# Cross-attention of a decoder layer: heads on 64 array rows each, maxima alternating with scores, weighted sums two at a time, all batches written out

## The reference, cut to what matters

```python
x = x + attn(layernorm(x), wq, wk, wv, wo)                 # 2 heads of 64, rotary, causal, 256 tokens
# cross-attention: B = 4, S = 256 queries, 1601 keys, 16 heads of 8
Q = split_heads(query @ Wq + bq); K = split_heads(key @ Wk + bk); V = split_heads(value @ Wv + bv)
scores = jnp.einsum('bhqd,bhkd->bhqk', Q, K) / sqrt(8)
attn = jax.nn.softmax(scores, axis=-1)
ctx = jnp.einsum('bhqk,bhkd->bhqd', attn, V)
x = x + (ctx.transpose(0, 2, 1, 3).reshape(4, 256, 128) @ Wo + bo)
x = x + ffn(layernorm(x), W1, b1, W2, b2, scale)           # 512 hidden, gelu, a low-rank term of the tokens
```

## Time and profile before

| what | value |
|---|---|
| time of three executions | 507.9, 504.13, 505.81 us, median 505.81 us |
| span of the profiled execution, first to last instruction | 502.5 us (its own device time is not given apart) |
| busy PE / DVE / ACT / POOL | 447.6 / 351.7 / 299.8 / 58.1 us |
| instructions | 10204 |
| mean granted TensorE clock | 0.929 of full |

### The profile page before, as it was taken

One profiled execution on the slowest core, in us unless ns is written; L12 is line 12 of the kernel. 1 busy time (PEld: TensorE's weight loads), 2 busy tenths in 40 slices (PEclk: granted clock), 3 DMA queues, 4 the chain that ended last, 5 costly groups with the idle time before them and its releaser, 6 DMA issues.

```text
span 502.5 us, 10204 instructions
## 1 busy us (share of the span) xinstructions
PE 447.6 (89%) x3264; PEld 197.8 (39%) x3264; DVE 351.7 (70%) x829; ACT 299.8 (60%) x608; POOL 58.1 (12%) x55
## 2 busy tenths in 40 slices
PE   1755899999899998999999997999999999999956
PEld 1542133445333434455333334455333435333224
DVE  3773988885969784786978882876878886892041
ACT  1411057676576756586677746586677648778811
POOL 3500000370000000460000000460000000000000
PEclk9856579999999999999999999999999999999956
DMA  6064720042032201051141202051140200000000
GB/s 223 3 223 127 207 90 2 1 149 99 27 117 70 74 5 47 34 191 57 31 142 39 77 1 82 1 198 50 33 151 30 77 1 12 1 2 0 1 0 12
DMA packets 18884, 33.80 MB, mean 67 GB/s; under 512 B 1424, under 2 KB 16400, under 8 KB 18832
## 3 DMA queue, kind: packets, MB, share of 16 engines
q1 hardware_dynamic: 18832, 33.10, 20.1%
HBM read 17.33 MB, written 11.93 MB: 58 GB/s over the span
## 4 chain that ended last, share of the span: by engine, by line
PE 68%; DVE 16%; issue 6%; DMA 5%; ACT 3%; SPq 1%; POOL 1%; DVEq 0%; POOLq 0%; ACTq 0%
PE wsum L976 18%; PE score L994 17%; PE ring L1010 15%; DVE part_max L634 8%; DMA q_unit<-q_rows 2%; PE ring L1145 2%; PE ring L1114 2%; PE ring L1107 2%; PE ring L1053 2%; DMA q_rows<-q_parts 2%; PE ring L1043 2%; PE ring L1021 1%; PE ring L1150 1%; PE ring L1157 1%; PE ring L1137 1%
## 5 line engine op out<-in xcount | busy, mean ns | idle before, releaser
L634 DVE TENSOR_REDUCE part_max<-ring 128x1 f32<-128x401 f32 x512 | 260.6, 567 | 81.4 <-PE ring L1010 80.2
L848 ACT ACTIVATE probs<-score 128x512 f32<-128x512 f32 (+1 forms) x416 | 224.8, 598 | 71.4 <-PE score L994 70.1
L1010 PE MATMUL ring<-k_unit,q_unit 96*128 96x401 bf16 x512 | 143.1, 355 | 7.2 <-DMA q_unit<-q_rows 6.3
L994 PE MATMUL score<-q_unit,k_unit 128*128 128x512 bf16 (+1 forms) x416 | 128.6, 390 | 5.4 <-issue 5.0
L976 PE MATMUL wsum<-probs,v_unit 128*32 128x256 f32 (+1 forms) x1664 | 130.6, 391 | 0.6 <-ACT q_unit L859 0.6
L1010 PEld LDWEIGHTS ring<-k_unit,q_unit 96*128 96x128 bf16 x512 | 48.6, 100 | 96.4 <-issue 25.5
L976 PEld LDWEIGHTS wsum<-probs,v_unit 128*32 128x32 f32 (+1 forms) x1664 | 34.2, 108 | 64.5 <-issue 42.0
L994 PEld LDWEIGHTS score<-q_unit,k_unit 128*128 128x128 bf16 (+1 forms) x416 | 31.6, 100 | 68.1 <-ACT probs L848 49.2
L859 ACT ACTIVATE q_unit<-ring 3x1024 bf16<-3x1024 bf16 x16 | 16.3, 1017 | 31.4 <-PE ring L1021 30.9
L595 POOL TENSOR_TENSOR var<-mv,c_sb 128x2 f32<-128x2 f32 x4 | 0.8, 197 | 228.7 <-DVE mv L784 228.7
L563 POOL TENSOR_TENSOR k_parts<-k_full,c_sb 128x802 bf16<-128x802 f32 x7 | 10.7, 1524 | 132.9 <-ACT k_full L894 132.9
(11 more groups left out here) (105 smaller groups left out, 316.0 us busy)
## 6 DMA issues: line engine op xcount, KB each, us to landing
k_unit<-k_rows SPq DMA_DIRECT2D x32, 300.2 KB
v_unit<-v_aug SPq DMA_DIRECT2D x16, 234.0 KB, 5.7
ctx_sb<-ctx_t SPq DMA_DIRECT2D x4, 800.5 KB, 6.3
k_rows<-k_parts SPq DMA_DIRECT2D x4, 601.5 KB, 3.3
k_rows<-k_parts SPq DMA_DIRECT2D x4, 599.2 KB, 3.7
k_rows<-k_parts SPq DMA_DIRECT2D x4, 401.0 KB, 4.1
k_rows<-k_parts SPq DMA_DIRECT2D x4, 399.5 KB, 4.3
q_unit<-q_rows SPq DMA_DIRECT2D x32, 48.0 KB
```

The source lines that it names most:

```text
L634: v_.tensor_reduce(part_max[:, par, q, head, hp, c:c + 1], ring[s][:, 0:CW], AX.X, ALU.max)\
L848: a_.activation(probs[0:rows, i % PB, :], score[i % EB][0:rows, :], ACT.Exp)\
L994: mm(score[i % EB][0:keys, :], k_unit[:, u, L * hp + P * t:L * hp + P * t + keys], q_unit[:, u, :, hp, :], start=True, stop=True).then_inc ...
L1010: mm(ring[s][:, 0:CW], q_unit[0:PR, mu, par, hp, P * q:P * (q + 1)], k_unit[0:PR, mu, L * hp + (CW - 1) * c:L * hp + (CW - 1) * c + CW], s ...
```

## The change

The pair of heads is pulled apart. Each half of the array's rows takes one head: rows 0 to 50 and 64 to 114 hold three rows of ones or maxima (`MR`) and the 48 rows of parts. `q_unit` loses its zero blocks. A score step is four matmuls of 256 columns on 51 rows in place of two of 512 on 128; a bank now has both pairs for one head half. Before each score pair stands one M on the other half of the rows. The weighted sums of two keys steps stand together (`PV_AT`). The numbers of M by keys step and unit change (`PAIRS`, `AHEAD`). The rows of ones are loaded once from DRAM, where VectorE set 32 rows of each unit before; the maxima rows of `q_unit` are zeroed by two small DMAs at each load of queries, because the M of a unit reads them too. The hardware loop is gone: all 16 units are written out.

```diff
-AHEAD = (4, 8, 8, 8)
-PR = 2 * TR
+MR = 3
+KR = MR + TR
+HALF = P // 2
-QUOTA = [[5, 5, 5, 5, 4, 4, 4], [5, 5, 5, 5, 4, 4, 4], [6, 6, 6, 4, 2, 0, 4], [7, 7, 6, 6, 2, 4, 4]]
+AHEAD = (4, 16, 14, 8)
+PAIRS = ((1, 1, 1, 1, 1, 1, 2, 1, 1, 1, 1, 1, 2), (1,) * 13,
+         (1, 1, 1, 2, 1, 1, 1, 2, 1, 1, 1, 1, 0), (2, 2, 1, 2, 2, 1, 2, 2, 1, 2, 2, 1, 2))
+TURN_AT = (10, 10, 11, 10)
+PV_AT = {1: (-2, -1), 3: (0, 1), 5: (2, 3), 7: (4, 5), 9: (6, 7), 11: (8, 9), 12: (10,)}
...
+    for t in range(KT):
+        pairs = PAIRS[u][t]
+        for n in range(2):
+            plan += todo[:min(pairs, 1)]
+            todo = todo[min(pairs, 1):]
+            plan.append(("S", v, t, n))
+        plan += todo[:2 * pairs - 2] if pairs > 1 else []
...
+        for at in PV_AT.get(t, ()):
+            if at >= 0:
+                plan.append(("PV", v, at))
+            elif v:
+                plan.append(("PV", v - 1, KT + at))
...
-                    sp.dma_start(q_unit[TR * par:TR * (par + 1), u, par, :, :].rearrange("p h n -> p (h n)"),
+                    sp.dma_start(q_unit[HALF * par + MR:HALF * par + KR, u, :, :].rearrange("p h n -> p (h n)"),
                                  q_rows[b, :, at:at + 2 * DX, :].rearrange("t (d h) n -> t d (h n)", h=2))\
                         .then_inc(unit_in[u], 16)
+                    sp.dma_start(q_unit[HALF * par:HALF * par + MR, u, :, :].rearrange("p h n -> p (h n)").bitcast(F32),
+                                 consts[0:MR, C_COLS["zeros"][0]:C_COLS["zeros"][1]]).then_inc(unit_in[u], 16)
...
-                v_.memset(k_unit[PR:P, u, :].bitcast(F32), TWO_ONES)
-                v_.memset(q_unit[:, u, :, :, :].rearrange("p a h n -> p (a h n)").bitcast(F32), 0.0)\
-                    .then_inc(unit_set, 1)
...
+            def scores(v, t, par):
+
+                u, i = v % UB, score_index(v, t, par)
+                keys = P if t < KT_FULL else LAST
+                rows = slice(HALF * par, HALF * par + KR)
...
+                if i >= EB:
+                    pe.wait_ge(probs_done, i - EB + 1)
+                for hp in range(2):
+                    last = mm(score[i % EB][0:keys, S * hp:S * (hp + 1)],
+                              k_unit[rows, u, L * hp + P * t:L * hp + P * t + keys], q_unit[rows, u, hp, :],
+                              start=True, stop=True)
+                last.then_inc(scores_ready, 1)
+
+            def maximum(item):
+
+                v, k = item[1:]
+                u = v % UB
+                hp, q, c, head = k // (2 * QT * KC), k // (2 * KC) % QT, k // 2 % KC, 1 - k % 2
+                if k == 0:
+                    pe.wait_ge(unit_in[u], 96 * (v // UB + 1))
...
+                s = take(item)
+                rows = slice(HALF * head, HALF * head + KR)
+                mm(ring[s][:, 0:CW], q_unit[rows, u, hp, P * q:P * (q + 1)],
+                   k_unit[rows, u, L * hp + (CW - 1) * c:L * hp + (CW - 1) * c + CW], start=True, stop=True)\
+                    .then_inc(filled[s], 1)
```

669 lines of the change are left out of this document (278 added, 391 removed), and 7 rows, old and new, of tables (PREP_END, PREP_SIDE).

## The result

The changed kernel takes 522.62 us (median of five executions, 518.69 to 530.3), the kernel before 505.81 (five, 503.9 to 507.9): a ratio of 1.032, 95% interval 1.025 to 1.040. It is slower, where 468 us and faster had been forecast. The profiled execution is the longest of the five (530.3 us, span 528.3); in the four others the span was 516.7 to 524.7 us and the mean granted clock 0.841 to 0.862, against 0.835 in the profiled one. What follows accounts for that execution: it is 25.8 us longer than the profiled one of the kernel before (span 502.5), where the medians are 16.8 apart.

A forecast was written before the change was run, and what follows sets the result against it. TensorE was taken as the bound, DVE near. From 502.5 us: three batches -29.7, first unit -4.1, last three -7.0, start +3.0 gave a 464.7 us span; plus 3.3 to the median, 468 us, 80% range 444 to 491.

The forecast's parts named there:

- Row halves: TensorE's keys step: maxima run beside scores on the other row half, so both cost 0.45 us, not 0.88.
- load rival: Keys step: if a weight load's 99 ns is a rate, six loads make it 0.60 us; 482 us, chance 0.12.
- serial rival: Row halves run one after the other on TensorE; a unit's core is 18.7 us; 490 us, chance 0.10.
- Joined sets: Weighted sums in pairs: some 0.2 us saved per avoided return, 7 returns a unit in place of 12 or 13.
- core of 13.3 us: TensorE's scores, maxima and weighted sums in a unit, side work excluded: 13.3 us, 6.6 less than 19.9.
- drift of "some 2 us": Four ring banks and three score banks let the engines drift by only some 2 us.
- rival with chance 0.07: Clock falls to 0.50 part of the time in unit 3: some 3 us a batch, more in unit 2; 478 us.
- unit 0 at 25 us: Unit 0, with the feed-forward: floors TensorE 22.6, DVE 22.3, ACT 20.2 us, plus an allowance for side work, 25 us.
- wait for the queries: Unit 2: TensorE waits 4.7 us for the query chain, 11.2 us long with two more DMAs.
- Loops and code: Both loop returns go, one a 3.38 us stop of TensorE; longer unrolled code costs 0.
- Start and first unit: Start: -2.4 for VectorE's settings, +1.5 for zero DMAs, +3.9 for eight more M; first unit 18.5 us, -4.1.
- Last three units: No side work, ACT's 15.4 us binds: 16.7, 16.2 and 14.4 us, -7.0.

The follow-up runs named there:

- the earlier tables: Side work of unit 0's tail and unit 2's query chain placed one keys step earlier; on the changed kernel, nothing else, 500.16 us (0.992).

## Why the prediction was wrong, point by point

**Row halves: right.** Pairs of scores with a maximum between start 0.23 us apart (217.01 to 217.24), where 0.22 had been forecast, and scores and maxima of a step take 0.50 us to the sums where nothing waits (212.19 to 212.69), against 0.45. The load rival and the serial rival are both out: three weight loads of 0.10 us each (the PEld row above, and the maxima's 99 ns) lie in a slot of 0.23, so they are not done one after the other with nothing beside them. The Trainium skill says so in another section of "TensorE: Matmul & The Clock Gate" than the one that the prediction weighed: by "The mechanism", a load runs beside a matmul when it aims at other row groups; the trace agrees.

**Joined sets and the core of 13.3 us: a term of the sum that was too small.** Sixteen weighted sums take 1.00 us as forecast. But the sum put 0.90 us of scores and maxima before them and named the score banks only as a drift of "some 2 us". With four pairs for three banks the block waits for ScalarE and takes 1.46 us. A unit's core is 6.5 x 2.46 = 16.0 us, 2.7 over the forecast; whole rows with pairs need 17.2. Much of the wait hides in busy time, since a maximum runs beside it. Single sums, which the prediction counted as a loss of 0.2 us each, bring the core to 6.5 x 2.14 = 13.9 us. But that is not the main error: at full clock the units show only some 5 us of it in the whole kernel.

**The clock: the step that failed.** The sum took nearly all of TensorE's work between start and end at full clock (0.5 us in unit 2 was all it added to a batch), and left the rest to a rival with chance 0.07. That rival was given 3 us a batch and more in unit 2, 10 over the forecast in all; the account above has 49.1 us, five times as much. It was also put mainly in the wrong unit: unit 3 ran at 1.00 in two batches of three, with TensorE busy 18.72 of 21.31 us. The clock fell in units 2 and 0 and in the last one. By unit, the profiled span is 63.6 us over the forecast's 464.7: unit 0 has 33.9 of that in its three batches, unit 1 14.4, the last three units 9.5, unit 2 9.3, the start with the first unit 4.4; unit 3 is 6.0 shorter than forecast and the end 1.8. Unit 0 shows the course (TensorE's timeline, then windows of 1 us):

```profile
187.87 0.44 PE L914 MATMUL ring<-c_sb,xn 128*128 128x128 f32 x2 [2.10 <-DVE xn L670]
```
```profile
188.00:189.00 1.00, 1.00 (x8) 0.60 (x9) 0.00 (x0) 0.38 (x1) 0.00 (x0) 0.78 0.00 0
189.00:190.00 1.00, 1.00 (x7) 0.42 (x7) 0.13 (x1) 0.00 (x0) 0.00 (x0) 0.50 0.00 0
...
204.00:205.00 1.00, 1.00 (x4) 0.79 (x3) 0.00 (x0) 0.30 (x1) 0.00 (x0) 0.50 0.00 0
205.00:206.00 1.00, 1.00 (x6) 0.56 (x4) 0.00 (x0) 0.54 (x2) 0.00 (x0) 0.69 0.00 0
```

TensorE waits 2.10 us for VectorE's layer norm, the clock falls to its lower level, 1.2 GHz, and stays there for 17 us (188.56 to 205.62), in which TensorE is busy nearly all the time. The wait alone is not the cause. The kernel before waited 1.05 us at this place and ran at 0.99, but whole rows in the new order waited 1.93 and held 1.00 in two batches of three, and halves with single sums waited 2.53 and held 0.89 to 0.94. The same kind of wait is followed by a long fall where the halves and the pairs stand together. The prediction had unit 0 at 25 us, measured 35.8 to 36.9: with 11.3 us three times, the largest single error, and up to 8 of the 11.3 are the clock's, since with the earlier tables the same pairs took 28.36 us at 1.00.

**The other units.** Unit 3 was forecast at 23.5 and took 21.3 to 21.9. Unit 2: forecast 26, measured 28.2 to 30.5, at clock 0.78 to 0.82; the wait for the queries was oversized (2.67, 1.95 and 0.69 us, forecast 4.7 a batch; of the 12.7 us for `q_unit<-consts` in the row of L889 7.4 lie in the start), and the unit is longer all the same. Unit 1: forecast 26.5, measured 31.2 to 31.5 at clock 1.00, and between 30.8 and 33.3 in every version since, whole rows too, but for the 35.0 with three ring banks. The first unit 1 of the changed kernel, at clock 1.00, shows where it goes if each stretch of TensorE's timeline is given to what started it: scores, maxima and sums 14.4 us and 1.6 idle ahead of them, side work 14.1 and 0.9 idle. The prediction had 13.3 for the first and 11.7 for the side work (25 less 13.3). The side work was 12.7 us in the kernel before, in the first unit 1, at clock 1.00; taking "some 2" off another unit 1 for its clock had made it too small, and in the new order it takes more. Single sums with the earlier tables save 1.3 us of scores and maxima here, but the sums cost 0.7 more and the side work 0.6 more, and TensorE waits 1.70 us for VectorE before a maximum; so unit 1 is no shorter. Start and first unit: 92.7 us against 88.3. Last three units: 56.8 against 47.3; 7.4 of it is the last one, at clock 0.53 (the same instructions took 14.87 us at 1.00 in the run with maxima on the same half).

**Loops and code.** The returns went, and no unit shows TensorE waiting for code: right.

**What was refuted, and what stays open.** Refuted: that the wait for the queries is what costs the time in the changed kernel, that two tiles side by side pull the clock down, that the new order costs. Shown: with pairs and the old tables the halves lose by clock and idle time more than they gain in work, pairs of sums cost on halves, earlier side work pays in the three layouts tried, and more columns on the idle half, or more rows, take 24 to 38 us off the half-clock time of the profiled executions once the long waits are shorter. Only argued: that the lower density of work is why the clock falls more easily on halves. Pairs against singles with the earlier tables is 116 against 106 us of half-clock time in the profiled executions, and over all of them 110 to 143 against 101 to 133, which does not prove that bursts matter for the clock; with the old tables it is 143 to 174 against 120 to 137. Whether a fourth score bank beside four ring banks would repair the pairs could not be tried, since all eight are in use.

## What to carry to other kernels

A change that joins steps of one engine into blocks has to be priced with the banks that the block fills: four results for three banks put the consumer's time inside the block, and of the 6.6 us forecast for a unit's core 3.9 were left. When TensorE's work shrinks while its waits for other engines stay, count the clock before the gain: find TensorE's waits in the old profile, and either move their producers ahead or allow for a stretch at half speed behind them. Cross the parts of a compound change (here layout, grouping and tables), since the same edit took 17 us off in one layout and added 12 in the other.

## What the runs showed of the hardware

TensorE can be busy nearly all the time and stay at 1.2 GHz: 20.14 of 21.82 us in the last unit at 0.53. The timeline of that unit:

```profile
484.61 1.94 PE L858 MATMUL wsum<-probs,v_unit 128*32 128x256 f32 x16
486.48 1.03 PE L873 MATMUL score<-q_unit,k_unit 51*128 51x256 bf16 x6
487.83 0.60 PE L873 MATMUL score<-q_unit,k_unit 51*128 51x256 bf16 x2 [0.32 <-ACT probs L729]
488.37 1.93 PE L858 MATMUL wsum<-probs,v_unit 128*32 128x256 f32 x16
```

Two keys steps take 3.76 us (484.61 to 488.37), with one wait of 0.32 in them, and the scores on 51 rows are alone on the array. With the scores run twice the unit ran at 1.00 and took 17.28 us. "TensorE: Matmul & The Clock Gate" in the Trainium skill, section "HAM oscillation — how this bites in real kernels", puts such falls down to idle gaps while data is awaited. The fall in unit 0 agrees in so far as it comes 0.7 us behind a wait of 2.10 us (the gaps of the page's example are longer); the time spent at the lower level almost without gaps, 16.1 of 17.0 us busy from 188 to 205, does not follow from it.

Executions of one kernel differ with the clock. The whole-row version with earlier tables took 493.3 to 495.0 us in four runs, with its clock at 1.00 between start and end; the one on halves with single sums took 483.5 to 496.0, at granted clocks of 0.895 down to 0.865. The kernel before, on whole rows, took 499.6 to 509.8 in thirteen runs beside the latter, at 0.938 down to 0.919. Where unit 0's table alone was earlier, the same unit took 27.9 and 31.9 us in one execution (at 1.00 and 0.84).
